# Two routings on TensorE's prefix sums, gathers eight tiles ahead, a shared network in the tail, and 161 products that nobody reads

## The reference

```python
x = x + attention0(layernorm(x), ctx)     # 16 heads of 16, one shared key and value head
x = x + moe0(layernorm(x))                # 8 experts of hidden size 1024, top 2
x = x + attention1(layernorm(x), ctx)     # one head of 256
x = x + moe1(layernorm(x))                # 8 experts of hidden size 256, top 2, and a shared one

# moe0: every token's row goes through its two experts
h = silu(xf @ gate[e].T) * (xf @ up[e].T)
out += mask[:, e] * (h @ down[e].T) * mean_w[e]    # mean weight of the tokens of e
# moe1: the row is scaled by its score before the expert, and added to
# hs = silu(xt @ w1s) * (xt @ w3s);  out = hs @ w2s
```

## Time and profile before

| | us |
|---|---|
| median of three executions (892.64 to 896.9) | 894.09 |
| the profiled execution, its own time | 895.82 |
| its span | 893.7 |
| TensorE, VectorE, ScalarE, GpSimd busy | 737.9, 604.2, 490.6, 301.2 |
| TensorE busy in 260 to 600 us, at a granted clock of 1.00 | 336.7 |
| mean granted clock | 0.913 |
| TensorE's last product ends | 868.2 |

### The profile page before, as it was taken

One profiled execution on the slowest core, in us unless ns is written; L12 is line 12 of the kernel. 1 busy time (PEld: TensorE's weight loads), 2 busy tenths in 40 slices (PEclk: granted clock), 3 DMA queues, 4 the chain that ended last, 5 costly groups with the idle time before them and its releaser, 6 DMA issues.

```text
span 893.7 us, 13789 instructions
## 1 busy us (share of the span) xinstructions
PE 737.9 (83%) x4852; PEld 643.3 (72%) x4852; DVE 604.2 (68%) x1093; ACT 490.5 (55%) x826; POOL 301.2 (34%) x309
## 2 busy tenths in 40 slices
PE   3999999962399999999999999992487677898960
PEld 3566676651399999999998999992365577788850
DVE  4766645367677878787867868774477784676744
ACT  1366556321356767767766767671564533676740
POOL 7266446410203131222221312110711031677850
PEclk9999999985599999999999999997678968899995
DMA  5000000010556767776858867555100172778848
GB/s 162 1 1 0 1 25 24 1 36 11 219 195 206 242 223 240 245 266 195 286 176 263 264 213 250 199 167 186 50 0 1 65 250 62 237 234 246 258 140 287
DMA packets 54437, 136.90 MB, mean 153 GB/s; under 512 B 6881, under 2 KB 23650, under 8 KB 54370
## 3 DMA queue, kind: packets, MB, share of 16 engines
q1 hardware_dynamic: 46882, 115.57, 39.2%
q0 software_dynamic: 7488, 20.46, 7.1%
HBM read 117.39 MB, written 18.61 MB: 152 GB/s over the span
## 4 chain that ended last, share of the span: by engine, by line
PE 51%; DVE 15%; issue 11%; POOL 10%; DMA 7%; ACT 5%; SPq 1%; POOLq 0%; DVEq 0%; ACTq 0%
PE ps L318 46%; POOL p_lo L644 4%; DVE w_lo L1138 4%; DMA xnb<-xm_d,gat 3%; ACT w_hi L749 2%; POOL y_d L732 1%; PE ps L2093 1%; DMA wr<-in_w1gu 1%; DMA wr<-in_w 1%; DMA h_lo<-y_d 1%; POOL a_lo L623 1%; DVE h_lo L1138 1%; POOL xnb L723 1%; PE ps L2049 1%; PE ps L1774 1%
## 5 line engine op out<-in xcount | busy, mean ns | idle before, releaser
L1138 DVE TENSOR_TENSOR w_lo<-wr,w_hi 128x1024 fp32r<-128x1024 f32 (+2 forms) x193 | 221.4, 1160 | 48.1 <-ACT w_hi L749 47.3
L749 ACT ACTIVATE w_hi<-wr 128x1024 fp32r<-128x1024 f32 (+2 forms) x193 | 192.1, 1000 | 38.1 <-DMA wr<-in_w 27.7
L318 PE MATMUL ps<-xe_hi,w_hi 128*128 128x256 f32 x600 | 174.2, 290 | 4.9 <-DVE xe_lo L1138 2.6
L318 PE MATMUL ps<-xe_lo,w_hi 128*128 128x256 f32 x600 | 171.8, 286 | 0.0
L318 PE MATMUL ps<-xe_hi,w_lo 128*128 128x256 f32 x600 | 171.7, 286 | 0.0
L665 POOL DMA_INDIRECT y_d<-ye,sca x39 | 43.4, 1113 | 279.0 <-ACT ye L898 274.4
L318 PE MATMUL ps<-w_hi,h_hi 128*128 128x256 f32 x422 | 126.1, 299 | 9.9 <-DVE h_lo L1138 6.9
L318 PEld LDWEIGHTS ps<-xe_hi,w_hi 128*128 128x128 f32 x600 | 117.2, 195 | 7.9 <-DVE xe_lo L1138 5.4
L318 PE MATMUL ps<-w_lo,h_hi 128*128 128x256 f32 x422 | 121.1, 287 | 0.0
L318 PE MATMUL ps<-w_hi,h_lo 128*128 128x256 f32 x422 | 121.0, 287 | 0.0
L318 PEld LDWEIGHTS ps<-xe_lo,w_hi 128*128 128x128 f32 x600 | 117.3, 196 | 0.0
(11 more groups left out here) (330 smaller groups left out, 1504.7 us busy)
## 6 DMA issues: line engine op xcount, KB each, us to landing
wr<-in_w SPq DMA_DIRECT2D x144, 512.0 KB, 4.5
wr<-in_w1gu SPq DMA_DIRECT2D x24, 512.0 KB, 4.9
wr<-in_w1d SPq DMA_DIRECT2D x24, 256.0 KB, 3.3
wr<-y_d SPq DMA_DIRECT2D x8, 512.0 KB, 5.8
x_all<-in_x SPq DMA_DIRECT2D x4, 512.0 KB, 5.6
xn_d<-xnb SPq DMA_DIRECT2D x4, 512.0 KB, 2.9
h_hi<-y_d SPq DMA_DIRECT2D x4, 512.0 KB, 8.5
h_lo<-y_d SPq DMA_DIRECT2D x4, 512.0 KB, 8.7
```

Source lines behind the costliest of these rows:

```text
L318: return nc.tensor.matmul(out, w, x, start=start, stop=stop, skip_group_check=True)
L749: return s.activation(o, i, ACT.Copy)
L1138: return v.tensor_tensor(o, a, b, ALU.subtract)
```

## The change

The prefix sums over the tiles go to TensorE: `msk` gets a row of zeros, and `count` adds each tile's sum to all later tiles, in two parts, the first inside the attention's loop. `place` reads the counts from PSUM. In layer 0 ScalarE multiplies the one-hots by the token's number (`tokens`). `tables` is four steps, not six or seven. x's normed rows are stored twice, so that a gather index needs no wrapping. SyncE issues the first two weight blocks and then waits for the first tile's rows. In layer 1 groups 2 and 3 of the shared network move behind the expert network, gathers go eight tiles ahead into a ring of eight, the second routing is placed before the shared network's gate, and the late rows land in other buffers. The norm's epsilon and its shift move from GpSimd to VectorE. Between all this TensorE gets 161 products of 512 columns whose results nothing reads.

```diff
 RING = 4
-AHEAD = 5
+XRING = 8
+AHEAD = 8
...
-        msk = sb("msk", [P, NT, E], bf16)
+        msk = sb("msk", [P, NT + 1, E], bf16)
...
+            def tokens(r):
+                for h in range(NG):
+                    act.wait_ge(r["tile"], at(r, "tile") + h + 1)
+                    for c in range(2):
+                        for t in range(h * GT, (h + 1) * GT):
+                            ins = s.activation(oha[:, c, t, 0:COLS], oh_a[:, c, t, 0:COLS], ACT.Copy, scale=tok1[:, c, t:t + 1])
+                    ins.then_inc(r["tok"], 1)
...
                 w0_hi(0, b)
-            x_hi0(0)
+                if b == 1:
...
                 sp.wait_ge(nb["xn"], g + 1)
                 sp.dma_start(rows(xn_d, g), nb["x"][:, :, :]).then_inc(xn_st, 16)
+                sp.dma_start(rows(xn_d, g + NG), nb["x"][:, :, :]).then_inc(xn_st, 16)
...
-            for t, b in turns_w:
+            for n, (t, b) in enumerate(turns_w):
+                if n == 2:
+                    sp.wait_ge(f0["x_in"][0], moved(0))
...
             for t in range(T0):
+                if t == 1:
+                    sp.wait_ge(x1_in[0], ring_sum(0, XRING))
...
-                link(g.tensor_scalar(rs1[k][:, q, :], mv1[k][:, q, :, 1], EPS, None, ALU.add))
-                ins = g.tensor_tensor(rs1[k][:, q, :], rs1[k][:, q, :], mhalf[:, :], ALU.pow)
-                if k == "a":
-                    link(ins)
-                    link(g.tensor_tensor(nm1[:, q, :], mv1[k][:, q, :, 0], rs1[k][:, q, :], ALU.mult))
-                    ins = g.tensor_scalar(nm1[:, q, :], nm1[:, q, :], -1.0, None, ALU.mult)
-                ins.then_inc(n["rstd"], 1)
+                g.tensor_tensor(rs1[k][:, q, :], rs1[k][:, q, :], mhalf[:, :], ALU.pow).then_inc(n["rstd"], 1)
...
-                    pool.wait_ge(f1["xt_mm"], t - RING + 1)
+                if t >= XRING:
+                    pool.wait_ge(f1["xt_mm"], t - XRING + 1)
...
             exponents(r1, 1)
+            for g in range(NG):
+                scaled(g)
             gate_shared(1)
-            scaled(0)
-            shared_hi(1)
-            scaled(1)
-            scaled(2)
-            gate_shared(2)
-            scaled(3)
...
             w1_hi(0, 0)
-            shared_hi(2)
-            gate_shared(3)
+            shared_hi(1)
+            x1_hi(0)
+            w1_hi(0, 1)
             w1_hi(1, 0)
-            w1_hi(0, 1)
-            x1_hi(0)
             x1_hi(1)
-            shared_hi(3)
...
+            gate_shared(2)
+            shared_hi(2)
+            gate_shared(3)
+            shared_hi(3)
...
-                dve.wait_ge(r["mm"], 1)
-                link(v.tensor_copy(tot[:, :, :], ps[:, (0, 7)[n], P:2 * P].rearrange("p (t e) -> p e t", e=E)))
...
+                counted = ps[:, (0, 6)[n], 0:(NT + 1) * E].rearrange("p (t e) -> p t e", e=E)
+                dve.wait_ge(r["mm"], at(r, "mm") + 1)
+                link(v.tensor_tensor(cmp_b[:, :, :, :], counted[:, NT, :].rearrange("p (o e k) -> p o e k", o=1, k=1
+                                                                                    ).to_broadcast([P, 2, E, E]),
                                      step_b[:, :, :, :], ALU.is_gt))
...
-                link(v.scalar_tensor_tensor(d_e[:, :], d_e[:, :], float(FT),
-                                            cum[:, :, NT - 1:NT].rearrange("p e o -> p (e o)"), ALU.mult, ALU.subtract))
-                link(v.tensor_tensor(d_e[:, :], d_e[:, :], n_e[:, :], ALU.add))
-                link(sub(cum[:, :, :], cum[:, :, :], tot[:, :, :]))
-                link(v.tensor_tensor(cum[:, :, :], cum[:, :, :], b_tile(d_e[:, :], NT), ALU.add))
-                link(v.tensor_tensor(slot[:, :, :], ps[:, (0, 7)[n], 0:P].rearrange("p (t e) -> p t e", e=E),
-                                     cum[:, :, :].rearrange("p e t -> p t e"), ALU.add))
+                link(v.scalar_tensor_tensor(slot[:, :, :], b_row(d_e[:, :], NT), float(FT), counted[:, 0:NT, :], ALU.mult, ALU.add))
                 link(v.tensor_tensor(tmp3[:, :, :], slot[:, :, :], b_row(from_e[:, :], NT), ALU.is_ge))
                 link(v.tensor_tensor(tmp3[:, :, :], tmp3[:, :, :], b_row(move_e[:, :], NT), ALU.mult))
                 link(v.tensor_tensor(slot[:, :, :], slot[:, :, :], tmp3[:, :, :], ALU.add))
-                for c in range(2):
-                    link(v.tensor_tensor(key[:, :, :], oh[:, c, :, :], slot[:, :, :], ALU.mult))
-                    link(v.tensor_reduce(slot2[:, c, :], key[:, :, :], AX.X, ALU.add))
+                link(v.tensor_tensor(picked[:, :, :, :], oh[:, :, :, :],
+                                     slot[:, :, :].rearrange("p (o t) e -> p o t e", o=1).to_broadcast([P, 2, NT, E]), ALU.mult))
+                link(v.tensor_reduce(slot2[:, :, :], picked[:, :, :, :], AX.X, ALU.add))
...
+                def tile_hots(h):
                     ts = slice(h * GT, (h + 1) * GT)
                     for c in range(2):
-                        ins = v.tensor_tensor(oh_a[:, c, ts, 0:w], b_row(iota_h[:, 0:w], GT), b_tile(sa_f[:, c, ts], w),
+                        ins = v.tensor_tensor(oh_a[:, c, ts, 0:COLS], b_row(iota_h[:, 0:COLS], GT), b_tile(sa_f[:, c, ts], COLS),
                                               ALU.is_equal)
+                    if n == 0:
+                        ins.then_inc(r["tile"], 1)
+                        return
                     link(ins)
                     for c in range(2):
-                        v.tensor_tensor(oha[:, c, ts, 0:w], oh_a[:, c, ts, 0:w], b_tile(tok1[:, c, ts], w), ALU.mult)
+                        v.tensor_tensor(oha[:, c, ts, 0:COLS], oh_a[:, c, ts, 0:COLS], b_tile(tok1[:, c, ts], COLS), ALU.mult)
...
+                def lane_hots(h):
+                    ts = slice(h * GT, (h + 1) * GT)
                     for c in range(2):
                         ins = v.tensor_tensor(ohb[n][:, c, ts, :], b_row(iota_p[:, :], GT), b_tile(sb_f[:, c, ts], P), ALU.is_equal)
                     ins.then_inc(r["hot"], 1)
+                tile_hots(0)
+                for h in range(NG):
+                    if h + 1 < NG:
+                        tile_hots(h + 1)
+                    lane_hots(h)
...
-                link(v.tensor_reduce(eid_b[:, :, :], cmp_s[:, :, :, :], AX.X, ALU.add))
-                link(v.tensor_tensor(eid_f[:, 0:T0], eid_b[:, 0, :], eid_b[:, 1, :], ALU.min))
-                v.tensor_copy(eid[n][:, :], eid_f[0:1, :]).then_inc(r["eid"], 1)
-                if n == 0:
...
+                link(v.tensor_reduce(eid_f[:, :], cmp_s[:, :, :, :].rearrange("p k t e -> p t k e"), AX.XY, ALU.add))
+                v.tensor_scalar(eid[n][:, :], eid_f[0:1, :], -float(E - 1), None, ALU.add).then_inc(r["eid"], 1)
+            def tables(n, r):
+                found = ps[:, (2, 6)[n], 256:256 + COLS]
+                dve.wait_ge(r["inv"], at(r, "inv") + 1)
+                v.tensor_scalar(gat[n][:, 0:COLS], found, -1.0, 0.0, ALU.add, ALU.max).then_inc(r["tab"], 1)
+                link(v.scalar_tensor_tensor(unused[:, :], found, 0.0, pad1[:, :], ALU.is_equal, ALU.mult))
+                v.scalar_tensor_tensor(sca[n][:, 0:COLS], found, -1.0, unused[:, :], ALU.add, ALU.add).then_inc(r["tab"], 1)
...
-                ins.then_inc(n["var"], 1)
+                link(ins)
+                v.tensor_scalar(rs1[k][:, q, :], mv1[k][:, q, :, 1], EPS, None, ALU.add).then_inc(n["var"], 1)
+            def shift_of(g):
+                dve.wait_ge(na["rstd"], NG + g + 1)
+                if g >= 2:
+                    dve.wait_ge(na["xn"], NG + g - 1)
+                v.scalar_tensor_tensor(nm1[:, g % 2, :], mv1["a"][:, g % 2, :, 0], -1.0, rs1["a"][:, g % 2, :], ALU.mult, ALU.mult
...
-            add_rows(0)
+            add_rows(0, 0)
+            add_rows(0, 1)
             statistics1(na, "a", 0)
-            add_rows(1)
+            add_rows(1, 0)
+            shift_of(0)
+            add_rows(1, 1)
             statistics1(na, "a", 1)
+            shift_of(1)
...
+            place(1, r1)
+            tables(1, r1)
             gated(1)
-            place(1, r1)
             add_shared(0)
-            tables(1, r1)
-            shared_lo(1)
-            gated(2)
-            add_shared(1)
...
+            for t in range(T0):
+                tile1(t)
+                if t == 0:
...
+            gated(2)
             shared_lo(2)
             gated(3)
+            add_last(0)
             add_shared(2)
-            dve.wait_ge(sgu_mm, KC * 2)
-            w1_lo(1, 0)
-            dve.wait_ge(sgu_mm, KC * NG)
-            w1_lo(0, 1)
-            x1_lo(0)
-            x1_lo(1)
             shared_lo(3)
+            add_last(1)
+            dve.wait_ge(so_ok, 2 * (NG - 1))
+            add_last(2)
             add_shared(3)
...
+            dve.wait_ge(so_ok, 2 * NG)
+            add_last(3)
...
+            def idle_products1(k):
+                for _ in range(k):
```

(68 more changed lines are left out.)

187 lines of the change are left out of this document (92 added, 95 removed).

## The result

The changed kernel took 861.98 us (median of 4; 861.19 to 863.74) and the one before 895.5 us beside it (median of 4): a ratio of 0.963, 95% interval 0.960 to 0.966, so 33.5 us less. On two chips of the later runs the ratio was 0.967 (0.964 to 0.969) and 0.967 (0.964 to 0.970), 30.0 and 27.9 us less. The forecast was 855 us, range 840 to 873. The profiled execution took 862.12 us at a span of 860.4, 33.3 less than before, at a mean granted clock of 0.958 in place of 0.913.

The account below looks back on a forecast made before the run. The prediction took VectorE to bound the first routing and GpSimd to pace the second network. Its terms, -8.5 - 5 - 31.7 + 5.7 = -39.5 us from the median of 894.09, gave 855 us, range 840 to 873 for 8 in 10.

Parts of the forecast that it names:

- First routing, -8.5: First routing and first network's start: faster transposes, placing, one-hots and tables, earlier gather and weights, 8.5 us less.
- Between the layers, -5: First network's end to layer 1's attention: higher TensorE clock and shorter norm steps, 5 us less, bounds -1 and -9.
- The hold: Between the layers: the 66 unread products cost TensorE 2.5 us before it can turn to the normed rows.
- the rival's 11 us more: Between the layers: unread products staying at 0.50 start the attention 11 us later; 868 us in all, chance 0.08.
- Second routing, -7.2: Second routing: placing starts 3.8 us earlier and is 2.5 shorter, so the first gather comes 7.2 us earlier.
- Start of the network, -12.3: Second network, first gather to first scatter: shared groups 2 and 3 leave the start, 12.3 us less.
- Second network, -12.2: Second network, first scatter to last scatter's end: eight tiles ahead leave GpSimd fewer operations, 12.2 us less.
- 63 x 1.44 = 90.7, with 5 us of waits: Second network: 63 GpSimd operations of 1.44 us plus 5 us of waits make 96 us, in place of 108.2.
- the rival of a slower GpSimd: Second network: denser work slows GpSimd to 1.72 us an operation, 18 us come back, 873 us; chance 0.11.
- The tail, +5.7: After the last scatter: VectorE's queue makes the tail 27.9 us in place of 22.2, 5.7 more.
- No gain from the level at all: TensorE's clock level: only the moved work pays, -2 and -4 are lost, 861 us; chance 0.07.
- Slower: Second network: gathers eight tiles ahead crowd the weights' loads, at 3 us a tile 927 us; chance 0.04.

Follow-up runs that it names:

- e5: The changed kernel, unedited, as yardstick in the second group of runs: 863.01 us, 0.967 of the kernel before.
- e6: The changed kernel with 52 more unread products in TensorE's idle time of the second routing: 861.35 us, 0.965 of the kernel before.
- e9: The changed kernel, unedited, as yardstick in the third group of runs: 864.67 us, 0.967 of the kernel before.
- e10: The changed kernel without any of the 161 unread products, run beside the unedited changed kernel: 870.70 us, 0.974 of the kernel before.
- e12: The changed kernel with e8's tail, 12 unread products in the second routing and tile 0's gate and up before tile 1's transposes: 859.34 us.
- e2: The changed kernel without the unread products between the layers and in layer 1's attention, keeping the first routing's: 0.980 of the kernel before.
- e1: The changed kernel without any of the 161 unread products, on the first group's slower chip: 0.980 of the kernel before.
- e7: The changed kernel with groups 2 and 3 of the shared network back ahead of the first tile: 871.52 us, 0.976 of the kernel before.
- e8: The changed kernel with the tail's additions reordered and group 1's adds given to GpSimd: 859.86 us, 0.963 of the kernel before.
- e3: The changed kernel with gathers five tiles ahead in place of eight, on the first group's slower chip: 0.972 of the kernel before.
- e4: The changed kernel with three landing buffers for the second network's weights in place of two: 0.973 of the kernel before.

## Why the prediction was right, step by step

- **First routing, -8.5:** -9.1 by the end of the first network. The first gather was forecast 7.7 us earlier and came 8.1 earlier once the 2.8 us are taken off that the two executions differ by before the transposes. Placing 4.86 us for 5.0, the scalings 0.222 us for 0.25, TensorE's third quarter at 240.82, where 243.5 less those 2.8 is 240.7, and what it waited for is the product that the prediction named. (The part left to VectorE was written as 4 x 1.7; its own terms, 0.60 and 1.20, give 4 x 1.8. The sum goes by ScalarE, so nothing changes.) No run put the old placing, the old tables or the old one-hots back: this part, and the second routing's, rest on the durations in the profiles.
- **The 2.8 us** were in no forecast, and seem to be luck of the profiled executions. At about 170 us (the same reciprocal of VectorE), where the kernels differ only in a few instructions of the set-up and in SyncE's second store of the normed rows, the profiles of before, after, e5, e6, e9, e10 and e12 stand at 173.3, 170.5, 170.9, 173.1, 170.5, 172.2 and 171.5; all but the first have the same instructions up to there. In 20 to 40 us the granted clock is 0.91 in before and e10 and 0.85 in e6, 1.00 in after, e5, e9 and e12. The Trainium skill ("TensorE: Matmul & The Clock Gate", Part 1) says that the moment at which the level rises differs from run to run of one kernel; these agree.
- **Between the layers, -5:** -2.2. The hold was sized at 2.5 (2.2 measured), the gain behind it at 7.4 (6.0 measured by the runs without the products). The prediction's own terms for this stretch, 1.2 us by the norm's steps, 7.4 and -2.5, add up to 6.1 and not to the 5 that it took. The 1.2 was not tested by itself; without the products the profiles stood hardly better there than before (90.5, 90.3 and 88.0 us in e10, e2 and e1 from the last scatter to the mask, 88.9 before). The hold of 2.2 us is the forecast's own 2.5; the rival's 11 us more did not come.
- **Second routing, -7.2:** -7.1. **Start of the network, -12.3:** -12.9, with gate and up 8.9 us behind the first gather (9.2 forecast). e7 shows that the move gives it, and more (17.1).
- **Second network, -12.2:** -4.6; here lies the error. The step was "63 x 1.44 = 90.7, with 5 us of waits". An operation did take 59.40 / 54 + 0.3 = 1.40 us (the rival of a slower GpSimd had 1.72), so 63 of them 88; the 5 us of waits were 15, most of them for ScalarE's copies of results (in 735 to 830 us 8.1 and 6.4 in the waits above). The prediction's own rows could have told: 68 x 1.44 = 97.9 of the 108.2 us before already leave 10 us of waits, so GpSimd did not pace the stage alone, and halving them had no ground. Five ahead, TensorE waits for gathered rows and the stage takes 107.4 us; eight ahead it waits for none, and the stage falls only to 102 to 104, whatever else is changed outside it (after, e5, e6, e8, e9, e10, e12: 102.1 to 103.6; 100.9 in e7). What holds it there is not shown by an experiment. The profile's chain names the loop of weight load, ScalarE's copy and VectorE's difference; the waits among TensorE, ScalarE and VectorE are the other candidate. The 24 tiles that were put at "some 4.0" take 4.3.
- **The tail, +5.7:** +5.4. VectorE's queue has a share in it, as e8 shows: 4.9 us taken off it shorten the tail by 2.6.
- **No gain from the level at all** was put at +6 and is what e10 measured: +6.0. The late loads of *Slower* are there in small: ScalarE waits 8.1 us for them in 735 to 830 us, 0.3 a tile, where it waited 1.5 before (768 to 863 us), and the chain above runs through them. With five ahead it is 6.5 us, so the three tiles more are not the main reason.
- **The whole:** 33.5 us less beside a forecast of 39.5, and 30.0 and 27.9 on the two later chips. The time lay well inside the range because the second network's miss (7.6 us) and that between the layers (2.8) were, in the profiled execution, partly paid for by the 2.8 us that no step had.

## What to carry to other kernels

When the engine that seems to pace a stage is relieved, the stage falls only to the next loop, of engines or of loads, so price that loop by its own measured time per tile and not as a few microseconds of waits. Products that nobody reads pay where the engine would wait anyway and real work follows at once at the higher level; where they start at the low one they last longer (7.16 us for 20 in e6, where the 22 ahead of them took 5.17), and either way they can hold the queue (2.2 us between the layers, 1.5 in e6). What is moved out of the start of a stage into a tail was worth its whole length here (17.1 us by e7, 16.7 of TensorE's work), less what it adds in the tail (5.7).

## What the runs showed of the hardware

- Executions of the same instructions stood up to 3.0 us apart at 170 us (170.5 in after and e9, 173.5 in e3); the ones ahead had a granted clock of 1.00 in 20 to 40 us, where e3 had 0.91.
- Behind 66 products that nobody reads the level is 1.00 when real work starts (layer 1's transposes, 8 in 1.03 us). It falls in the 32 small one-hot products all the same: in e6 it was 1.00 until 696 us, 0.97 in 696 to 700 and 0.50 in 700 to 704.
- On one of the three chips of e1 to e12, ScalarE and VectorE stood idle for 4 to 9 us while TensorE went on with gaps of about 1 us (e2, with the transfer engines at 0.96 in 722 to 726 us), and no packet that loads instructions moved in that time in e2 and e4; the cause stays open.
- VectorE's two differences of two SBUF tiles took 3.73 us in place of 1.28 beside GpSimd's adds, and the second ended 0.54 us behind the add that had started before it.
